# Two multi-head attention blocks of a one-core kernel: a pipeline one step shorter, the output copy in two halves, and the norm's work at other places of a step

## The reference

```
x = layernorm(x + L0 attention(x))     16 heads of 8, softmax over all 256 keys
x = layernorm(x + L0 mixture(x))       8 experts, 2 chosen for each token
x = layernorm(x + L1 attention(x))     one head, softmax over the queries
x = layernorm(x + L1 mixing(x))
x = layernorm(x + L2 attention(x))     16 heads of 8, causal
x = layernorm(x + L2 mixing(x))
x = layernorm(x + L3 attention(x))     linear attention
x = layernorm(x + L3 mixture(x))       16 experts, 1 chosen
```

```
q = (x @ Wq.T + bq);  k = (x @ Wk.T + bk);  v = (x @ Wv.T + bv)      per head of 8
w = softmax(q k^T / sqrt(8));  out = (w v) @ Wo.T + bo
logits = x @ router_w;  top 2, softmax of the two;  each token's row goes to two experts
```

## Time and profile before

| | us |
|---|---|
| runs shown | 1440.7, 1450.24, 1440.87 |
| median | 1440.87 |
| profiled execution, its own time | 1446.28 |
| its span | 1444.5 |
| mean granted TensorE clock | 0.846 of full |
| L0 attention | about 15 to 385 us of the span |
| L2 attention | about 732 to 1049 us |

### The profile page before, as it was taken

The page is one execution under the profiler, slowest core; times in us unless marked ns, Lnnn a source line. Parts: engine busy times, 40 slices in busy tenths (PEclk is TensorE's granted clock), DMA queues, the critical chain, the costliest instruction groups (busy, mean ns, idle before and its releaser), DMA issues.

```text
span 1444.5 us, 32880 instructions
## 1 busy us (share of the span) xinstructions
PE 1101.5 (76%) x9370; PEld 711.7 (49%) x9399; DVE 901.7 (62%) x3421; ACT 633.1 (44%) x1432; POOL 402.5 (28%) x638
## 2 busy tenths in 40 slices
PE   4998898887299994776758997999866997429940
PEld 1344343333188883664535554555455665326730
DVE  2788777794323334996745775777467788752237
ACT  2577666664144441335413665665553322103410
POOL 4002322333434554233420000000034111442553
PEclk9999888897599996997656999999975898558985
DMA  5323223211556677211012221221010100134523
GB/s 148 76 75 80 76 70 83 71 33 39 160 176 206 202 201 235 77 44 30 22 44 68 65 66 47 65 66 34 18 38 21 31 22 8 56 106 110 166 70 94
DMA packets 158713, 119.17 MB, mean 83 GB/s; under 512 B 16513, under 2 KB 146818, under 8 KB 158466
## 3 DMA queue, kind: packets, MB, share of 16 engines
q1 hardware_dynamic: 151426, 103.29, 25.8%
q0 software_dynamic: 7168, 14.37, 2.9%
HBM read 47.26 MB, written 23.41 MB: 49 GB/s over the span
## 4 chain that ended last, share of the span: by engine, by line
PE 48%; DVE 22%; issue 12%; ACT 6%; POOL 5%; DMA 4%; SPq 2%; DVEq 1%; another core or an unknown queue 1%; POOLq 0%; ACTq 0%
PE po L467 7%; PE po L1506 7%; DVE mx L646 4%; PE pm L432 4%; PE pt L1500 4%; PE pm L1500 3%; PE pm L419 3%; DVE xg L336 3%; PE p L564 2%; PE p L388 2%; ACT ob L601 2%; POOL rstd L329 2%; DMA xs<-xg 2%; ACT ex L592 1%; POOL sorted L1340 1%
## 5 line engine op out<-in xcount | busy, mean ns | idle before, releaser
L646 DVE TENSOR_REDUCE mx<-pm 128x2 f32<-128x512 f32 (+1 forms) x512 | 303.9, 619 | 154.4 <-PE pm L445 76.2
L592 ACT ACTIVATE ex<-pt 128x512 f32<-128x512 f32 (+1 forms) x512 | 264.9, 547 | 180.5 <-PE pt L438 107.8
L326 POOL TENSOR_SCALAR ve<-mv 128x2 f32<-128x2 f32 x96 | 25.5, 265 | 748.1 <-DVE mv L320 748.1
L432 PE MATMUL pm<-ks,qs 64*128 64x256 bf16 (+1 forms) x1024 | 177.4, 265 | 13.4 <-DVE mx L646 9.4
L467 PE MATMUL po<-ex,va 128*32 128x256 f32 (+1 forms) x2048 | 159.7, 385 | 21.1 <-ACT ob L601 15.1
L438 PE MATMUL pt<-qs,ks 64*128 64x256 bf16 (+1 forms) x1024 | 168.6, 257 | 2.7 <-issue 2.1
L1583 POOL DMA_INDIRECT result<-ye,to_row x128 | 122.5, 957 | 153.1 <-issue 108.3
L432 PEld LDWEIGHTS pm<-ks,qs 64*128 64x128 bf16 x1024 | 74.9, 99 | 100.3 <-issue 55.9
L1506 PE MATMUL po<-he,we 128*128 128x256 f32 (+1 forms) x448 | 112.9, 395 | 0.6 <-DVE yt L1544 0.4
L310 ACT COPY xt<-p 128x256 f32<-128x256 f32 x112 | 41.8, 373 | 154.7 <-PE p L306 126.9
L419 PE MATMUL pm<-hide_q,half_id 64*128 64x256 bf16 (+1 forms) x512 | 88.2, 258 | 11.7 <-issue 4.9
(11 more groups left out here) (281 smaller groups left out, 2427.6 us busy)
## 6 DMA issues: line engine op xcount, KB each, us to landing
we<-in_pack SPq DMA_DIRECT2D x40, 514.5 KB
xs<-xg SPq DMA_DIRECT2D x112, 128.0 KB
qs<-parts SPq DMA_DIRECT2D x192, 64.0 KB
ks<-parts SPq DMA_DIRECT2D x192, 64.0 KB
we<-in_pack SPq DMA_DIRECT2D x16, 512.0 KB
xe<-sorted SPq DMA_DIRECT2D x56, 132.0 KB
yr<-result SPq DMA_DIRECT2D x48, 128.0 KB, 2.2
xr<-xg SPq DMA_DIRECT2D x32, 128.0 KB, 2.2
```

Source lines behind the costliest of these rows:

```text
L432: last_m = pe.matmul(mine[:, e * S + k0:e * S + k1], queries, keys[:, k0:k1], start=not causal, stop=e == 1 or not causal)
L592: nc.scalar.activation(ex[j % 2][:, :, :].rearrange("p (e g) k -> p g e k", g=2)[:, 1 - u, :, lo:S], pt[:, u, :].rearrange("p (b k) -> p b ...
L646: nc.vector.tensor_reduce(mx[q.slot % 2][:, qt, u, 2 * b:2 * b + 2], pm[:, u, :].rearrange("p (b k) -> p b k", k=S)[:, :, 0:hi], AX.X, ALU ...
```

## The change

- The max pass runs under `at(1)` from place 1 on, one step earlier. Everything that comes after it moves one step earlier too: the exp pass to `at(2)`, the output copy, the norm and the router. Each `sweep` has one lag less (L0: TensorE and VectorE 9 to 8; L2: 6 to 5). In L2 this leaves four steps ahead of TensorE's loop and 12 for it, three rounds where there were two. In L0 it stays at two rounds. The stack transfers themselves are written as before.
- `po` is copied in two halves. The first bank's half is copied at place 1, the second's at place 5. `times_v` waits for the half whose bank it writes.
- The output product `y` moves from place 0.1 to place 4.0, and uses the other half of the bank `p1`, so it waits for the last split of q and k (`parts_sb`). `res` and the norm's statistics move on VectorE from place 0 to place 4, `norm_apply` from place 7 to 5. GpSimd computes `rstd` at the end of its step, not at the head.
- The router's product moves from place 4.1 to 5.1; the first two parts of `put` one place earlier.

```diff
-            sweep(sp, 7, step, lead=SLOTS if routed else 0)
+            sweep(sp, 6, step, lead=SLOTS if routed else 0)
...
                 if j == 0:
-                    wait(pe, o_sb, a + q.n)
+                    wait(pe, o_sb, 2 * (a + q.n) - 1)
+                if j == 4:
+                    wait(pe, o_sb, 2 * (a + q.n))
...
-                if (j, u) == (0, 1) and (q := at(5)):
-                    pe.wait_ge(ont_sb, a + q.n + 1)
-                    for t in range(2):
-                        last = pe.matmul(p1[:, t * P:t * P + P], ont[q.slot % 2][:, t * P:t * P + P],
-                                         mat(f"o{layer}"), start=True, stop=True)
-                    last.then_inc(y_ps, 1)
...
+                if (j, u) == (4, 0) and (q := at(4)):
+                    pe.wait_ge(ont_sb, a + q.n + 1)
+                    if at(0):
+                        pe.wait_ge(parts_sb, 3 * (a + at(0).n + 1))
+                    for t in range(2):
+                        last = pe.matmul(p1[:, S + t * P:S + t * P + P], ont[q.slot % 2][:, t * P:t * P + P],
+                                         mat(f"o{layer}"), start=True, stop=True)
+                    last.then_inc(y_ps, 1)
...
-                        scores(at(3) if j >= T0 else at(4), (j - T0) % 8, at(2) if j >= M0 else at(3), (j - M0) % 8, u)
+                        scores(at(2) if j >= T0 else at(3), (j - T0) % 8, at(1) if j >= M0 else at(2), (j - M0) % 8, u)
...
-            sweep(pe, 9 if routed else 6, step)
+            sweep(pe, 8 if routed else 5, step)
...
-                    if j == V0 and (q := at(4)):
-                        act.wait_ge(pv_ps, 8 * (a + q.n + 1))
-                        wait(act, ot_ps, a + q.n)
-                        nc.scalar.copy(ob[:, :, :], po[:, :, :].rearrange("p a (b k) -> p (a b) k", k=S)
+                    if j in (1, V0) and (q := at(3)):
+                        part = slice(0, 2) if j == 1 else slice(2, 4)
+                        act.wait_ge(pv_ps, 8 * (a + q.n) + (4 if j == 1 else 8))
+                        if j == 1:
+                            wait(act, ot_ps, a + q.n)
+                        nc.scalar.copy(ob[:, part, :], po[:, part.start // 2, :].rearrange("p (b k) -> p b k", k=S)
                                        ).then_inc(o_sb, 1)
...
-                    if j == 0 and (q := at(5)):
+                    if j == 4 and (q := at(4)):
                         norm_stats(dve, q, n)
...
-                    if j == 7 and (q := at(5)):
+                    if j == 5 and (q := at(4)):
                         norm_apply(dve, q, n)
...
-                if (q := at(5)):
-                    norm_rstd(pool, q, n)
...
                     scatter(pool, q, 1, xr[q.slot][:, 1], xs0)
+                if (q := at(4)):
+                    norm_rstd(pool, q, n)
```

127 lines of the change are left out of this document (63 added, 64 removed).

## The result

| | before | after |
|---|---|---|
| median of the runs made together, us | 1445.55 | 1461.32 |
| ratio, 95% interval | | 1.0103, 1.0063 to 1.0144 |
| profiled execution's span, us | 1444.5 | 1454.1 |
| mean granted TensorE clock | 0.846 | 0.856 |

What follows compares the result with a forecast made beforehand. L0's loaded periods lose to a full, then starved VectorE and a slowed TensorE; TensorE bounds L2. Terms -1 + 0.6 - 2.4 - 25.4 - 3 + 0 + 8 = -23.2 took 1440.9 to 1418 us, range 1408 to 1441.

Steps and rivals of the forecast that it cites:

- stop at place 3.1: L0's loaded periods: an unnamed wait, begun after GpSimd's second scatter, costs TensorE 1.4 us; half was expected back.
- loaded periods: Nine L0 periods with GpSimd's scatters running: 20.42 us each was to become 17.6, -25.4 us in all.
- residual, statistics and normed rows: Moved on VectorE toward its 1.69 us idle at place 5: about 1.9 us less between places 7 and 3.
- The output copy: One 1.01 us copy becomes two; TensorE's 0.53 wait goes, gaining 0.5 us a period, 0.4 at full clock.
- The stacks: SyncE's 13 issues per sequence, needed by the max pass, were to finish in time: cost nothing, cover 5 us.
- The clock: TensorE's clock in L0's loaded periods, mean 0.82 before, was assumed to hold, with periods at 1.00.
- the clock holds, the stop at place 3.1 is whole: Rival: loaded L0 periods last 19.0 us, gaining -12.8 instead of -25.4, so 1430 us; chance 0.15.
- The price of 1.25 for rstd: Normed rows' one unhidden wait for rstd, 1.25 us; taken as 0 if GpSimd is free by place 4.
- L0's other periods: Six L0 periods at full clock, before and after the loaded ones: 0.4 us less each, -2.4 in all.
- The branch: L2's TensorE loop takes its branch back twice instead of once: +8 us; no such pause in L0.
- The end of L0: Last four groups of scatters start earlier because rstd no longer stands ahead on GpSimd: -3 us.
- The slower rival: Norm chain's waits reach 1 us in 24 steps of L0 and L2, clock still falls: 1459 us; chance 0.07.

Runs made afterwards that it cites:

- best: Changed kernel with the norm's work at its old places and L2's TensorE loop run once, no branch back: 1419.5 us, 0.980 of the kernel before.
- rankfirst: Changed kernel with the normed rows at the end of VectorE's place 5, behind the copies of logits and ranks: 1423.6 us, 1.007 of the kernel before.
- loop1: Changed kernel with five more TensorE steps of L2 written out, so its loop takes no branch back: 1427.4 us, 1.008 of the kernel before.

## Why the prediction was wrong

Two steps of the prediction failed in the main. It gave back half of the stop at place 3.1 in the loaded periods, and it put the move of residual, statistics and normed rows at a net of nothing. The loaded periods were forecast at 17.6 and measured at 19.7, L2's period at 16.6 and 17.2.

*The output copy.* Right. Two copies of 0.59, no wait for either, and -0.48 us a loaded period (157.2 to 152.9) and -0.43 in L2 (16.57 to 16.14; 0.28 where the loop is written out too) against my 0.5 and 0.4 to 0.5.

*The stacks.* Costed at nothing, with 5 us of cover. That held in the changed kernel, beyond the first max pass of each block. It doesn't hold where the period is shorter: in L2 of the runs with the shorter pipeline and the norm at its old places single max passes wait up to 1.8 us for them.

*The clock.* Mostly right: 1.00 in four loaded periods and 0.92 in five, instead of mostly 0.82 to 0.84. The period hardly followed, because new idle time took the place of slow work.

*The stop at place 3.1.* "Half of the 1.4" is the first step that failed. It had no mechanism behind it, and the stop didn't give back any of it: it moved to place 2.1 with the sequence of GpSimd's work and stayed whole (1.63 on VectorE). At the level at which the result was measured this decides the loaded periods: with the stop and the norm at its old places ("best") one takes 19.8, in the changed kernel 19.4 to 20.1. Without the stop, at the lower level, the changed L0 has 160.9 for nine instead of 177.6: that is 16.7 of the 19.2 us that the nine are longer than forecast. Spacing the scatters takes it away, 1.6 to 2.5 us a period, more than the 1.4 that I read off TensorE's idle pieces, since ScalarE's and VectorE's late start and the clock behind it belong to it. The rival "the clock holds, the stop at place 3.1 is whole" had this mechanism, at 19.0 a period, which the periods at clock 1.00 have.

*Residual, statistics and normed rows.* The second step that failed, and the dearest in L2. I held each move against VectorE's idle time at place 5 and asked whether it fits; it fits, but the ranks and logits, which stand behind it at place 5, release the bank for TensorE's transposes at 6.0. That is 1.1 us in each loaded step. Without the stop the whole move costs 1.4 a period (148.3 to 160.9 for nine); with it the move makes no difference that these traces can tell. Where nothing was starved the price is bare: 1.09 us in each L2 period. I had put +0.7 for the late maxima against -0.5 for the copy and called it zero; the runs give +1.09 against -0.43 (16.57 to 16.14), which is the +0.66 of the trace. The price of 1.25 for rstd from the earlier trace rows was a bound that I cut to zero by the end of GpSimd's scatters; in L2 there are no scatters, only 1.2 us of GpSimd behind the statistics, and the wait was 0.57 in every period. VectorE waiting for rstd in every step was named in the prediction as a sign of being wrong altogether, and in L2 it is there.

*L0's other periods.* -2.4 became +3.8: the normed rows ahead of the ranks cost there too. The third is 18.0 instead of 17.0, and the thirteenth 18.65 instead of 16.58; with the ranks ahead (rankfirst) they are 17.0 and 16.8, where loop1 beside it has 18.0 and 18.6.

*The branch.* Right in kind: the two cost 12.2 us over the neighbouring periods in this trace (23.17 - 17.23 and 23.47 - 17.22), where the one before cost 8.1; in the other runs one costs 6.7 to 9.0. The reason for expecting none in L0 was that nothing stood idle behind its branch; the rows of the branch itself bear that out (0.25 us).

*The end of L0.* Wrong: rstd left the head, but the chain of the last scatters (now back to back only from 363.44 to 380.69) waits for VectorE's `place` instead (3.97 and 2.39 us ahead of two groups).

*The slower rival* named the chain "y, res, statistics, rstd, with the maxima queued behind", 1 us a step from 0.7 us on. That is what happened in L2. I gave it 0.07 since I let VectorE's idle time at place 5 speak against it, which I had read in L0 alone, and I tied it to a clock that falls, which it doesn't need. That its 1459 lies near the measured 1461 is luck: it has all nine loaded periods at the old clock and 24 us for 24 steps.

## What to carry to other kernels

An engine's idle time pays only for work whose followers on the same queue nobody waits for: before moving an instruction into a gap, list what stands behind it up to the end of the gap and who waits for that. Price a move in the stage without slack (L2 here), where it shows bare. Of this change the smallest part (a copy in two halves) gained in both blocks, the router's new places gained in L0 where no stop was in the way, and the shorter pipeline gained nothing that the runs can tell. The copy alone, with the branch of the loop avoided and the scatters apart, gives 0.966 of the time before.

## What the runs showed of the hardware

- Where GpSimd issues indirect transfers close together, the other engines can stop: with their four starts 1.3 us apart a loaded period took 22.4 us, with 2.0 us between the second and the third 19.8, with 1.6 to 3.8 us between all of them and at later places 17.3, for the same transfers. This was so in four groups of runs and not in two, where the second arrangement took 16.5. In the stop VectorE starts up to 1.8 us behind the start of the product that it waits for, instead of 0.43, while TensorE's own rows go on for a time. What passes between them isn't shown by any run.
- A branch back in TensorE's queue in L2, over a body of 2291 rows, costs 6 to 9 us. Of these 3.4 to 4.1 are the branch's own row, and the rest is a smaller idle and a low clock behind it. The same loop construct in L0, over 1650 rows, has a row of 0.25 us and no pause. That the length makes the difference fits every loop of the trace and wasn't tested.
